# Local attention: inverse norms as a power of -1/2 on GpSimd, one tile at a time; experts' running operations inside the combining loop

## Chip, cores and metric

One core of a Trainium2 chip runs the whole program. The metric is device time in microseconds (us) of one execution. Before the change it is 1561.78 us, the median of three runs (1561.13 to 1563.83).

## What is computed

The input `x` is (2, 1024, 256) in float32. The reference adds two blocks to it:

```python
x = x + experts(attention_0(x, cond), phi, W, b)      # soft mixture of 64 experts, 32 slots each
x = x + two_layers(quaternion_filter(x, cond), ...)   # two layers of local attention + feed-forward
```

In the experts, `combine` is a softmax over all 2048 slots, and the output is `combine @ y`. In each of the two layers, on 8 heads of 64:

```python
q, k, v = split(shift_token(x) @ wqkv)
q = q / clip(norm(q), 1e-12) * qs;  k = k / clip(norm(k), 1e-12) * ksc
q, k = rotary_xpos(q, k)                 # q*cos*scale + rotate_half(q)*sin*scale
sim = 8 * q k^T, in windows of 128 rows with the window before;  x = x + softmax(sim) @ v @ wo
x = x + ffn(layernorm(shift_token(x)))
```

## The kernel before

The program is a chain of stages with semaphores written out by hand; every engine runs a fixed order of instructions. Two stages are touched.

**Experts** (`stage_moe`). A loop of 4 chunks, 512 slots each. The softmax over slots is a running one: each chunk has new maxima (`nmc`), and `fac` is the factor by which what was summed so far is scaled. At the end of a chunk comes the combining loop over 16 tiles of 128 rows. For tile t TensorE (PE) does 12 products `ETs` x `ys` into a bank (L1076) and then 4 transposes of tile t+2 (L1016). ScalarE (ACT) copies those transposed rows (`ETs[0]`, L1118). VectorE (DVE) adds the bank to the running output `O` (L1188) and subtracts to get the low part of tile t+2's rows (`split_rows`, L1166), for which PE waits two tiles later. Between the last split of `ys` (L1175) and this loop DVE does three small running operations on 128x16: `nrun` <- `nmc` (L1182), `dtmp` <- `DEN` x `fac` (L1184), `DEN` <- `dtmp` + `dc` (L1185). `chain` puts a wait behind each for its own end. In the last chunk GpSimd (POOL) leaves the loop of chunks and works on weights of the next stage meanwhile (L1228 to L1242).

**Layers** (`stage_layers`). Attention works on 16 windows ("tiles") of 128 rows per layer, one per slot t, as a pipeline: in slot t PE transposes the rotated rows of tile t-2 (`rows_of`, L1614), makes queries and keys of tile t (L1587, 12 matmuls), scores of t-2 (L1628), transposes the probabilities of t-3 (L1650), projects t-4 (L1669), makes values of t (L1587, 6 matmuls) and applies the probabilities of t-3 (L1660). After queries and keys of tile t: ACT copies (`qkr`, L1816) and squares (`sq`, L1819); DVE sums the squares per head (`ss`, L1991) and multiplies by sines (`sinp`, L1985); POOL multiplies by cosines (`cosines`, L1494), adds (`turn`, L1502) and multiplies by the inverse norms `rn` (`normalised`, L1508). POOL also scales the probabilities (`probabilities`, L1485, two halves of a tile) and, in slots 6 to 11, takes low parts of the feed-forward weights (`low_piece`, L1457).

The inverse norms are made for two tiles at a time, in odd slots: DVE `tensor_scalar_max` (L1994), ACT `norms` with Sqrt (L1829), DVE `reciprocal` in `inverse_norms` (L1999). So `normalised` of an even tile t-1 runs in the odd slot t, behind `turn(t)`, and that of t behind the first half of the probabilities. Sqrt and Exp are in different table sets of ACT; the compiler puts an ACT_TABLE_LOAD at each switch. The first two tiles of layer 0 are done before its pipeline starts, those of layer 1 in the last unit of the feed-forward of layer 0 (`ahead`).

## Time and profile before

| | |
|---|---|
| median of three runs | 1561.78 us |
| the profiled execution | 1562.27 us |
| its span in the trace | 1560.5 us |
| mean granted TensorE clock | 0.988 |
| attention of layer 0 in the trace | about 903 to 1110 us |
| attention of layer 1 | about 1232 to 1454 us |
| combining loop of the last chunk | 832 to 870 us |

The span is one execution from first to last instruction; the profiled execution's own time has 1.8 us around it. "Idle before" is time of an engine in front of an instruction, with the instruction that released it. Starts are in us from the start of the span, durations in us in timelines and in ns as a mean of one in groups.

### The profile page before, as it was taken

To read this page: it belongs to the slowest core of one execution; us is meant where nothing else is said; L and a number is where in the kernel's file an instruction comes from. 1 tells how busy PE (TensorE), PEld (TensorE's weight loads), DVE (VectorE), ACT (ScalarE), POOL (GpSimd) and SP (SyncE) were. 2 spreads that over 40 slices of the span, in tenths; PEclk is the share of its full clock that TensorE was granted. 3 is DMA by queue.
4 is the path that set the end of the run, shared out by engine and by line. 5 is a ranking of instruction groups with operands and counts; after the bars stand their busy time and mean duration, and the time that the engine had idled before them with its cause. 6 is when DMAs were issued, how large, how long until landed. Compare 5 with 4: busy or idle time off the path is not lost. (4 is left out here: it accounts for less than half of the span.)

```text
span 1560.5 us, 24403 instructions
## 1 busy us (share of the span) xinstructions
PE 1470.8 (94%) x9004; PEld 964.0 (62%) x9004; DVE 1024.2 (66%) x1855; ACT 903.1 (58%) x1888; POOL 521.8 (33%) x323
## 2 busy tenths in 40 slices
PE   8889999999998899999998989999999889999998
PEld 3432222222225679797886668777777678777776
DVE  3768888888835446455565656666597566666675
ACT  5137777777784443435242277878543478978341
POOL 7100000000003400000004177887443478887222
PEclk9999999999999999999999999999999999999999
DMA  7920223110000312030304120000200100000010
GB/s 246 162 41 1 42 41 42 22 21 2 1 11 14 125 45 78 13 108 13 108 0 146 41 71 2 2 1 1 74 9 0 58 1 2 1 1 28 14 41 27
DMA packets 59476, 64.84 MB, mean 42 GB/s; under 512 B 15154, under 2 KB 48706, under 8 KB 59380
## 3 DMA queue, kind: packets, MB, share of 16 engines
q1 hardware_dynamic: 58020, 60.17, 15.4%
q10 hardware_dynamic: 1360, 3.41, 0.6%
q8 instruction: 58, 0.95, 0.2%
q14 instruction: 38, 0.31, 0.1%
HBM read 52.88 MB, written 10.49 MB: 41 GB/s over the span
## 5 line engine op out<-in xcount | busy, mean ns | idle before, releaser
L581 DVE TENSOR_REDUCE mcol<-bank 128x1 f32<-128x1024 f32 x256 | 302.1, 1217 | 59.0 <-PE bank L572 59.0
L669 ACT ACTIVATE a_pt<-bank 128x512 f32<-128x512 f32 x512 | 266.4, 602 | 89.2 <-PE bank L701 89.2
L701 PE MATMUL bank<-qa,ka 99*128 99x512 bf16 x512 | 193.7, 386 | 7.6 <-ACT a_pt L669 3.8
L572 PE MATMUL bank<-ka,qa 96*128 96x512 bf16 x512 | 193.2, 385 | 6.3 <-DMA ka<-k_parts 2.9
L2045 DVE CUSTOM_DVE_ANT_0 w_sm<-bank,mask 128x256 f32<-128x256 f32 (+1 forms) x256 | 88.8, 403 | 109.9 <-PE bank L1628 109.9
L1587 PE MATMUL bank<-wqkv,w_hst 128*128 128x512 f32 x576 | 153.6, 412 | 2.7 <-DVE w_sinp L1985 2.3
L701 PEld LDWEIGHTS bank<-qa,ka 99*128 99x128 bf16 x512 | 49.1, 98 | 165.7 <-ACT a_pt L669 121.3
L712 PE MATMUL bank<-a_pt,vst 128*32 128x512 f32 x1024 | 136.4, 605 | 0.1
L1879 ACT ACTIVATE w_sm<-w_sm,w_st 128x256 f32<-128x256 f32 (+1 forms) x256 | 123.9, 488 | 17.8 <-DVE w_st L2045 17.6
L1587 PEld LDWEIGHTS bank<-wqkv,w_hst 128*128 128x128 f32 x576 | 106.8, 193 | 26.6 <-issue 5.1
L1485 POOL TENSOR_TENSOR w_sm<-w_sm,w_st 128x1024 f32<-128x1024 f32 (+1 forms) x64 | 115.4, 1804 | 19.0 <-DVE w_st L2052 18.9
L618 POOL COPY vst<-v 128x512 f32<-128x512 f32 x8 | 4.9, 612 | 336.1 <-PE bank L712 279.6
L1076 PE MATMUL bank<-f_y,f_ET 128*128 128x256 f32 x768 | 110.4, 293 | 6.8 <-DVE f_ET L1166 6.1
L1076 PEld LDWEIGHTS bank<-f_y,f_ET 128*128 128x128 f32 x768 | 97.8, 194 | 10.2 <-DVE f_ET L1166 7.1
L1033 PE MATMUL bank<-phi,X0T 128*128 128x512 f32 x384 | 92.1, 395 | 4.6 <-PEq L768 4.6
L1494 POOL TENSOR_TENSOR w_cosp<-w_qkr,cosT 128x1024 f32<-128x1024 f32 x32 | 76.5, 2392 | 56.8 <-ACT w_qkr L1816 28.4
L1502 POOL TENSOR_TENSOR w_turned<-w_cosp,w_sinp 128x1024 f32<-128x1024 f32 x32 | 76.5, 2389 | 45.7 <-issue 43.1
L1007 PE MATMUL bank<-f_th,X 128*128 128x512 f32 x384 | 90.3, 389 | 0.0
L572 PEld LDWEIGHTS bank<-ka,qa 96*128 96x128 bf16 x512 | 49.8, 99 | 62.7 <-DVE mcol L581 11.3
L1033 PEld LDWEIGHTS bank<-phi,X0T 128*128 128x128 f32 x384 | 72.9, 191 | 20.7 <-issue 5.4
L742 POOL CAST phi<-phi 128x1024 fp32r<-128x1024 f32 x5 | 5.2, 1039 | 240.7 <-PE bank L1033 151.1
L1118 ACT ACTIVATE f_ET<-bank 128x512 fp32r<-128x512 f32 x64 | 37.8, 597 | 81.8 <-PE bank L1016 81.8
(254 smaller groups left out, 2867.2 us busy)
## 6 DMA issues: line engine op xcount, KB each, us to landing
f_wex<-in_W SPq DMA_DIRECT2D x8, 2048.0 KB, 12.0
qa<-q_parts SPq DMA_DIRECT2D x48, 128.0 KB, 4.8
ka<-k_parts SPq DMA_DIRECT2D x48, 128.0 KB, 5.0
q_parts<-p_parts SPq DMA_DIRECT2D x16, 192.0 KB, 3.2
k_parts<-p_parts SPq DMA_DIRECT2D x8, 384.0 KB, 3.4
wqkv_raw<-in_wqkv SPq DMA_DIRECT2D x2, 1536.0 KB, 6.5
w_raw<-in_w SPq DMA_DIRECT2D x2, 1408.0 KB, 5.9
phi<-in_phi SPq DMA_DIRECT2D x5, 512.0 KB, 3.7
```

Source lines behind the costliest of these rows:

```text
L572: last = nc.tensor.matmul(max_bank(G, r)[:, jh * HALF:(jh + 1) * HALF], G["qa"][k][0:KS, hg % 2, h, it * P:(it + 1) * P], G["ka"][k][0:KS, ...
L581: nc.vector.reduce_max(G["mcol"][hg % 2][:, p:p + 1], max_bank(G, r)[:, :], X).then_inc(G["max_free"], 1)
L669: nc.scalar.activation(pt[n % 2][:, q, :], sbank(HG * step + q), ACT.Exp, scale=HD0 ** -0.5).then_inc(p_ready, 1)
L701: mm(sbank(i), ka[k][:, q, n * P:(n + 1) * P], qa[k][:, ih, q, :], start=True, stop=True).then_inc(st_ps, 1)
L712: last = mm(obank[32 * q:32 * q + 32, :], vst[hg // 2 % 2][:, jt, q, :], pt[jt % 2][:, q, :], start=(jt == 0), stop=(jt == TT - 1))
L1007: last = mm(PB[2 + b][:, k * HALF:(k + 1) * HALF], X0[cx][:, b * TT + mt, k * P:(k + 1) * P], ths[ct][:, mt % 2, :], start=(mt == n == 0), ...
L1033: last = mm(logit_bank(mt)[:, b * HALF:(b + 1) * HALF], X0T[cx][:, k, b * T + mt * P:b * T + (mt + 1) * P], phis[cp][:, k, :], start=(n == ...
L1076: last = mm(PB[1][:, HALF * (t % 2):HALF * (t % 2) + D], ETs[ce][:, t % 2, n, :], ys[cy][:, n, t // TT, :], start=(n == i == 0), stop=(n = ...
L1485: V.tensor_tensor(sm[:, i % 2, hs, keys(i)], sm[:, i % 2, hs, keys(i)], st[:, i % 2, 3, hs].unsqueeze(2).to_broadcast([P, 4, 2 * WIN if i ...
L1587: last = mm(out_ps, hst[:, i // 2 % 2, ch, k, (i % 2) * P:(i % 2 + 1) * P], wqkv[cw][:, k, j * INNER:(j + 1) * INNER], start=(n == k == 0) ...
L1879: last = S(sm[:, i % 2, h, keys(i)], sm[:, i % 2, h, keys(i)], ACT.Exp, bias=st[:, i % 2, 1, h:h + 1], scale=-1.0, accum_out=st[:, i % 2, ...
L2045: V.tensor_tensor_reduce(sm[:, s, h, keys(i)], S_PS[h % 2][:, c0:c0 + 2 * WIN][:, keys(i)], mask_of(i), -QK_SCALE, HIGHEST, ALU.add, ALU.m ...
```

## The change

The three running operations of the experts go from in front of the combining loop to a place inside it, behind tile 12's addition and the split of tile 14. In the layers, Sqrt on ACT and the maximum and reciprocal on DVE (for two tiles) go; POOL does a maximum and a power with a constant tensor of -0.5 for each tile, directly behind `turn(t)`, and `normalised(t)` runs in slot t for each tile. DVE's sum of squares now waits that the power of two tiles before is done (`ss` has two buffers).

```diff
--- experts, DVE
                     link = chain(dve, run_step, 3 * c)
-                    dve.wait_ge(run_arg, c + 1)
-                    link(V.tensor_copy(nrun[:, 0, :], nmc[:, :]))
                     dve.wait_ge(run_fac, c + 1)
-                    link(V.tensor_tensor(dtmp[:, :], DEN[:, :], fac[:, :], ALU.mult))
-                    link(V.tensor_tensor(DEN[:, :], dtmp[:, :], dc[:, :], ALU.add))
                     for t in range(TILES):
...
                             split_rows(t + 2)
+                        if t == TILES - 4:
+                            link(V.tensor_copy(nrun[:, 0, :], nmc[:, :]))
+                            link(V.tensor_tensor(dtmp[:, :], DEN[:, :], fac[:, :], ALU.mult))
+                            link(V.tensor_tensor(DEN[:, :], dtmp[:, :], dc[:, :], ALU.add))
--- layers, POOL
+                    def inverse_norms(i):
+                        pool.wait_ge(ss_done, before(i) + 1)
+                        V.tensor_scalar_max(nsq[:, i % 2, :], ss[:, i % 2, :], 1e-24).then_inc(n_square, 1)
+                        pool.wait_ge(n_square, before(i) + 1)
+                        V.tensor_tensor(rn[:, i // 2 % 2, i % 2, :], nsq[:, i % 2, :], exponent[:, :], ALU.pow).then_inc(rn_done, 1)
...
-                        pool.wait_ge(rn_done, NG // 2 * l + i // 2 + 1)
+                        pool.wait_ge(rn_done, before(i) + 1)
...
                             cosines(t)
-                            if t == 1:
-                                normalised(t - 1)
                             turn(t)
-                        if there(t) and t % 2 and t > 1:
-                            normalised(t - 1)
+                            inverse_norms(t)
                         if there(t - 2):
                             probabilities(t - 2, 0)
-                        if there(t) and t % 2:
+                        if there(t):
                             normalised(t)
--- layers, ACT
-                def norms(l, q):
-                    act.wait_ge(n_square, NG // 2 * l + q + 1)
-                    act.wait_ge(rn_done, NG // 2 * l + q)
-                    S(nrm[:, :, :], nsq[:, :, :], ACT.Sqrt).then_inc(n_sqrt, 1)
...
-                        if there(t) and t % 2:
-                            norms(l, t // 2)
--- layers, DVE
                 def squared_norms(l, i):
                     dve.wait_ge(sq_done, NG * l + i + 1)
+                    dve.wait_ge(rn_done, NG * l + max(i - 1, 0))
                     V.reduce_sum(ss[:, i % 2, :], sq[:, :].rearrange("p (h d) -> p h d", d=HD1), X).then_inc(ss_done, 1)
-                    if i % 2:
-                        dve.wait_ge(ss_done, NG * l + i + 1)
-                        V.tensor_scalar_max(nsq[:, :, :], ss[:, :, :], 1e-24).then_inc(n_square, 1)
-
-                def inverse_norms(l, q):
-                    dve.wait_ge(n_sqrt, NG // 2 * l + q + 1)
-                    dve.wait_ge(turn_done, NG * l + max(2 * q - 2, 0))
-                    V.reciprocal(rn[:, q % 2, :, :], nrm[:, :, :]).then_inc(rn_done, 1)
```

POOL's order in slots 4 and 5 of layer 0 before (`w_cosp` is `cosines`, `w_turned<-w_cosp` is `turn`, `w_turned<-w_turned` is `normalised`, `w_sm` is `probabilities`):

```order
L1494 TENSOR_TENSOR w_cosp<-w_qkr,cosT 128x1024 [waits w_add_done,w_qk_sb]
L1502 TENSOR_TENSOR w_turned<-w_cosp,w_sinp 128x1024 [waits w_tk_ps,w_sin_done,w_cos_done]
L1485 TENSOR_TENSOR w_sm<-w_sm,w_st 128x1024 [waits w_d_done] x2
L1494 TENSOR_TENSOR w_cosp<-w_qkr,cosT 128x1024 [waits w_add_done,w_qk_sb]
L1502 TENSOR_TENSOR w_turned<-w_cosp,w_sinp 128x1024 [waits w_tk_ps,w_sin_done,w_cos_done]
L1508 TENSOR_TENSOR w_turned<-w_turned,w_rn 128x1024 [waits w_rn_done,w_add_done]
L1485 TENSOR_TENSOR w_sm<-w_sm,w_st 128x1024 [waits w_d_done]
L1508 TENSOR_TENSOR w_turned<-w_turned,w_rn 128x1024 [waits w_rn_done,w_add_done]
```

and the same two slots now (the first rows of the second slot are those of the first):

```order
L1494 TENSOR_TENSOR w_cosp<-w_qkr,cosT 128x1024 [waits w_add_done,w_qk_sb]
L1502 TENSOR_TENSOR w_turned<-w_cosp,w_sinp 128x1024 [waits w_tk_ps,w_sin_done,w_cos_done]
L1506 TENSOR_SCALAR w_nsq<-w_ss 128x16 [waits w_ss_done]
L1508 TENSOR_TENSOR w_rn<-w_nsq,w_exponent 128x16 [waits w_n_square]
L1485 TENSOR_TENSOR w_sm<-w_sm,w_st 128x1024 [waits w_d_done]
L1514 TENSOR_TENSOR w_turned<-w_turned,w_rn 128x1024 [waits w_rn_done,w_add_done]
L1485 TENSOR_TENSOR w_sm<-w_sm,w_st 128x1024 [waits w_d_done]
```

The even tile's `normalised` moved from the slot after it, behind that slot's `cosines` and `turn`, into its own slot.

DVE's order at the start of the combining loop before:

```order
L1175 TENSOR_TENSOR f_y<-bank,f_y 128x512
L1182 COPY f_nrun<-f_nmc 128x16
L88 ISA
L1184 TENSOR_TENSOR f_dtmp<-den,f_fac 128x16
L88 REGISTER_ALU
L1185 TENSOR_TENSOR den<-f_dtmp,f_dc 128x16
L88 REGISTER_ALU
L1188 SCALAR_TENSOR_TENSOR O<-O,f_fac,bank 128x256
```

and the place of the three operations now, near the loop's end:

```order
L1184 SCALAR_TENSOR_TENSOR O<-O,f_fac,bank 128x256
L1165 REGISTER_ALU
L1166 TENSOR_TENSOR f_ET<-bank,f_ET 128x512
L1190 COPY f_nrun<-f_nmc 128x16
L88 ISA
L1191 TENSOR_TENSOR f_dtmp<-den,f_fac 128x16
L88 REGISTER_ALU
L1192 TENSOR_TENSOR den<-f_dtmp,f_dc 128x16
```

They moved behind 13 of the loop's 16 additions and 13 of its 14 splits.

## Rows read from the trace of the kernel before

**Rows 1.** The page: busy time, share of the span, instructions.

```profile
PE 1470.8 (94%) x9004; PEld 964.0 (62%) x9004; DVE 1024.2 (66%) x1855; ACT 903.1 (58%) x1888; POOL 521.8 (33%) x323
```

**Rows 2.** Timeline of DVE, start of the last combining loop: start, us, instruction, idle before.

```profile
831.97 3.20 DVE L1182 COPY f_nrun<-f_nmc 128x16 f32<-128x16 f32 x1
...
838.58 1.37 DVE L1185 TENSOR_TENSOR den<-f_dtmp,f_dc 128x16 f32<-128x16 f32 x1
...
869.08 0.48 DVE L1188 SCALAR_TENSOR_TENSOR O<-O,f_fac,bank 128x256 f32<-128x256 f32 x1 [1.19 <-PE bank L1076]
```

**Rows 3.** The same of the chunk before: one of three alike, a step, the last addition.

```profile
748.60 0.17 DVE L1184 TENSOR_TENSOR f_dtmp<-den,f_fac 128x16 f32<-128x16 f32 x1
...
772.74 0.69 DVE L1166 TENSOR_TENSOR f_ET<-bank,f_ET 128x512 fp32r<-128x512 f32 x1 [0.59 <-ACT f_ET L1118]
...
777.10 0.48 DVE L1188 SCALAR_TENSOR_TENSOR O<-O,f_fac,bank 128x256 f32<-128x256 f32 x1 [1.20 <-PE bank L1076]
```

**Rows 4.** Timeline of POOL beside the last combining loop.

```profile
831.65 6.86 POOL L1231 TENSOR_TENSOR wqkv<-wqkv_raw,wqkv 128x1536 fp32r<-128x1536 f32 x2
...
844.99 1.28 POOL L1242 TENSOR_TENSOR sinT<-sinT,qks 128x512 f32<-128x512 f32 x1
```

**Rows 5.** Timeline of PE: the loop's start in either chunk.

```profile
748.54 0.62 PE L1076 MATMUL bank<-f_y,f_ET 128*128 128x256 f32 x3 [0.17 <-DVE f_y L1175]
...
832.11 0.63 PE L1076 MATMUL bank<-f_y,f_ET 128*128 128x256 f32 x3 [0.18 <-DVE f_y L1175]
...
841.12 2.93 PE L1076 MATMUL bank<-f_y,f_ET 128*128 128x256 f32 x12 [6.08 <-DVE f_ET L1166]
```

**Rows 6.** All instructions that touch `w_turned`: who waited for it.

```profile
  PE bank L1614: 21.5, 15
```

**Rows 7.** Timeline of PE: slots 3, 4, 16 of layer 0, slots 4, 6, 7 of layer 1.

```profile
921.66 0.66 PE L1660 MATMUL bank<-w_PT,w_vsb 128*64 128x128 f32 x8 [0.85 <-DVE w_PT L2058]
925.25 1.97 PE L1614 MATMUL bank<-ident,w_turned 128*128 128x128 f32 x8 [2.94 <-POOL w_turned L1508]
926.87 4.98 PE L1587 MATMUL bank<-wqkv,w_hst 128*128 128x512 f32 x12
...
1092.50 1.14 PE L1628 MATMUL bank<-w_kT,w_qT 64*128 64x256 f32 x8 [1.67 <-ACT w_qT L1860]
...
1259.15 4.43 PE L1587 MATMUL bank<-wqkv,w_hst 128*128 128x512 f32 x12
...
1286.55 1.09 PE L1614 MATMUL bank<-ident,w_turned 128*128 128x128 f32 x8 [0.96 <-POOL w_turned L1508]
1287.40 3.04 PE L1587 MATMUL bank<-wqkv,w_hst 128*128 128x512 f32 x12
...
1299.47 1.09 PE L1614 MATMUL bank<-ident,w_turned 128*128 128x128 f32 x8
```

**Rows 8.** Busy time by stretch; granted clock is the third number from the end.

```profile
925.00:941.00 16.00, 15.75 (x107) 13.08 (x108) 7.48 (x24) 8.77 (x23) 11.73 (x7) 0.81 0.00 1
```

**Rows 9.** Groups of POOL by line and shape: busy us, mean ns, idle before.

```profile
L1485 POOL TENSOR_TENSOR w_sm<-w_sm,w_st 128x1024 f32<-128x1024 f32 x56 | 106.4, 1900 | 17.6 <-DVE w_st L2052 17.5
L1494 POOL TENSOR_TENSOR w_cosp<-w_qkr,cosT 128x1024 f32<-128x1024 f32 x32 | 76.5, 2392 | 56.8 <-ACT w_qkr L1816 28.4 <-issue 28.4
L1502 POOL TENSOR_TENSOR w_turned<-w_cosp,w_sinp 128x1024 f32<-128x1024 f32 x32 | 76.5, 2389 | 45.7 <-issue 43.1 <-POOL w_cosp L1494 2.2
L1508 POOL TENSOR_TENSOR w_turned<-w_turned,w_rn 128x1024 f32<-128x1024 f32 x32 | 61.9, 1935 | 7.6 <-DVE w_rn L1999 7.4
L1457 POOL TENSOR_TENSOR w<-w_raw,w 128x704 fp32r<-128x704 f32 x8 | 14.4, 1795 | 0.0
...
L990 POOL TENSOR_TENSOR f_bias_rows<-f_bex,f_bias_part 16x256 fp32r<-16x256 f32 x4 | 2.9, 733 | 0.7 <-POOL f_bias_part L987 0.7
...
L975 POOL MEMSET f_nrun<- 128x16 f32 x1 | 0.1, 120 | 0.0
```

**Rows 10.** Groups of ACT from 882 to 1500 us: loads of tables.

```profile
L1829 ACT ACT_TABLE_LOAD x16 | 20.5, 1283 | 0.3
```

More of the change, by code:

```diff
@@ L1273, in stage_layers @@
         nsq = sb("w_nsq", [P, 2, 2 * H1])
-        nrm = sb("w_nrm", [P, 2, 2 * H1])
+        exponent = sb("w_exponent", [P, 2 * H1])
         rn = sb("w_rn", [P, 2, 2, 2 * H1])
@@ L1331, in stage_layers @@
             "step", "on_ready", "t_ps", "x1_done", "rot_ps", "rot_out", "zeroed"))
-        (h_high, h_low, qk_ps, v_ps, qk_sb, v_sb, sq_done, ss_done, n_square, n_sqrt, rn_done) = (sem("w_" + n) for n in (
-            "h_high", "h_low", "qk_ps", "v_ps", "qk_sb", "v_sb", "sq_done", "ss_done", "n_square", "n_sqrt", "rn_done"))
+        (h_high, h_low, qk_ps, v_ps, qk_sb, v_sb, sq_done, ss_done, n_square, rn_done) = (sem("w_" + n) for n in (
+            "h_high", "h_low", "qk_ps", "v_ps", "qk_sb", "v_sb", "sq_done", "ss_done", "n_square", "rn_done"))
         (cos_done, sin_done, add_done, turn_done, tq_ps, tk_ps, qT_done, kT_done, s_ps, s_masked, e_done,
@@ L1535, in _ @@
                 V.memset(eps[:, :], LN_EPS).then_inc(consts, 1)
-                pool.wait_ge(consts, 2)
+                V.memset(exponent[:, :], -0.5).then_inc(consts, 1)
+                pool.wait_ge(consts, 3)
                 attention(0)
@@ L1939, in feed_forward @@
                             round_qkv(l + 1)
-                        if ahead:
-                            norms(l + 1, 0)
                 for n in range(2):
@@ L1949, in _ @@
                         rotated(2)
-                norms(0, 0)
                 rotated(3)
@@ L2086, in attention @@
                             added(t - 4)
-                        if there(t) and t % 2:
-                            inverse_norms(l, t // 2)
                         if there(t - 3):
@@ L2133, in feed_forward @@
                             high(u + 1)
-                        if ahead:
-                            inverse_norms(l + 1, 0)
                         for m in range(KD):
@@ L2165, in _ @@
                 sines(0, 1)
-                inverse_norms(0, 0)
                 attention(0, EARLY_SLOTS)
```

## The prediction

> **What bounds the kernel now.** I read the page first: PE is busy for 94% of the span, no other engine for more than 66% [rows 1], so outside the places where PE stands still nothing is to be gained. The groups of instructions then show who made it stand: two places bear on the change.
>
> The first is the combining loop of the last chunk. The timelines of the two last chunks, side by side, are to be compared. In the third chunk the loop runs from 748.54 (its first product that waits, PE) to 777.10 (last addition of DVE), 28.56 us [rows 3, 5]; in the fourth from 832.11 to 869.08, 36.97 us [rows 2, 5]. The work is the same; 8.41 us are lost once. The reader sees where: the three running operations on 128x16 take 0.17 us each in the third chunk [rows 3], but in the fourth the first alone 3.20 us and all three 7.98 us (831.97 to 839.95) [rows 2]. POOL is at work on large tensors through just that stretch [rows 4], and nobody else is. DVE's next split comes late, and PE waits 6.08 us for it [rows 5]; the other 2.3 us follow while PE comes up to its clock again (12 products take 2.93 us).
>
> The second is the attention. All instructions on `w_turned` show that PE waits 21.5 us in 15 waits for `normalised` [rows 6]. The timeline shows the pattern: slot 6 of layer 1 begins with a wait of 0.96 us, slot 7 with none, and a slot without one is 12.92 us long (1299.47 - 1286.55) [rows 7]. Only even slots wait: the even tile's `normalised` stands on POOL behind `cosines` and `turn` of the tile after it. The slots 4 wait longest, 2.94 us each, and behind that the granted clock is 0.81 for 16 us, between the levels of 1.2 and 2.4 GHz [rows 8]; 12 matmuls take 4.98 us in layer 0 and 4.43 in layer 1, where they take 3.04 at full clock [rows 7].
>
> **Part by part.** The sum is made against the profiled execution, 1562.27 us (span 1560.5); the median is 0.5 lower.
>
> *A, experts: -8.4 us.* At tile 12 of the last loop the time is about 862 - 8, still past POOL's last operation (846.27) [rows 4], so the three take 0.17 each. In the loop DVE idles 0.59 us per tile before a split [rows 3]; three operations with their waits are some 0.6 us, once per chunk. That cover holds them; without it 4 x 0.6 = 2.4 us would be paid. The other DVE operations at the loop's start take one input from PSUM, and the split (0.69) and addition (0.48) show no stretching in either chunk. So the fourth loop becomes like the third: 8.41 us.
>
> The Trainium skill, in "SBUF — State Buffer", on the shared port pair, states that DVE and GpSimd take it as an exclusive lock for a whole instruction, and that DVE needs it for copies in a two-port mode and for two SBUF inputs. By that rule the operations are not slowed in proportion but wait out whole POOL instructions; the trace agrees (3.20 us beside operations of 3.43, 6.86 in two) [rows 2, 4], and the rule too frees them at the new place. It also says that the new small POOL instructions can be held up by DVE, which I price below from rows.
>
> *B, waits of PE for `normalised`: -21.5 us* [rows 6]. By the new order an even tile is ready about a whole slot earlier: in slot t `turn` ends, then come the norm, 1.90 of probabilities and 1.94 of `normalised` [rows 9], and PE wants it only two slot starts after its own slot began. That is a margin of some 10 us. What is late next is not this tile but the probabilities, under E.
>
> *C, clock: -4.5 us.* With the waits of 2.94 us gone the clock has nothing to fall for: 12 matmuls 4.98 - 3.04 and 4.43 - 3.04, the transposes ahead of them 1.97 - 1.09 and, in layer 1, some 0.3 [rows 7]: 1.94 + 0.88 + 1.39 + 0.3.
>
> *D, ACT and DVE: -3.3 us.* 16 groups of Sqrt lose a table load of 1.28 us each [rows 10] and 15 the load back; nearly all of the 40 us lie beside PE's work and give nothing. On the path are two places: DVE waits for the Sqrt in slot 3 and copies probabilities late, for which PE waits 0.85 us in each layer [rows 7], 1.7; and in slot 16, where PE has no projections to hide ACT's copies, it waits 1.67 us for `w_qT` [rows 7], of which I take half, 0.8 per layer, as ACT's backlog of exponentials and loads.
>
> *E, POOL's new work: +8.0 us.* Per tile a maximum and a power on 128x16. The trace has no power. Lower bound for each: 0.12 us, the memset of 128x16. Upper bound for the power: 1.94 us, a multiplication of 128x1024, that is, as if each of the 16 numbers took 64 plain operations. A short operation of two inputs with 256 columns takes 0.73 [rows 9]; I take 0.7 for the power, as it is nearest in kind, 0.12 for the maximum, and 0.17 for the wait between them (0.7 us of idle in 4 before L990). Together 1.0 us per tile. POOL's slot is then 2 x 1.90 + 2.39 + 2.39 + 1.94 = 10.5, now 11.5 us [rows 9]: hidden under 12.9. In slots 6 to 11 a low part (1.80) comes on top, 13.3 us against 12.9: 6 x 0.4 = 2.4. The first tile of the second sequence has one window of keys instead of two, which shortens PE's slot there more than POOL's; I add 1.2 for it and take 1 off for the margin that PE leaves before it wants the second half of the probabilities: 2.6 us per layer (an estimate). Slots 2 and 3 are short on PE and POOL is the slower one there; two norms push the probabilities of tile 1 some 1.4 us past PE's need: 1.4 per layer. So 2 x 4.0. With the power at 0.12 the whole of E is about 1 us; at 1.94 the excess of 1.24 counts in those six slots and the first two: 2 x (4.0 + 8 x 1.24), about 28.
>
> DVE's maximum and reciprocal (0.5 us for two tiles) go from beside PE's work: nothing. The new wait of the sum of squares is for a power two slots back: nothing, unless the power is of a slot's length. POOL's memset of the exponent is 0.12 us where POOL idles.
>
> Sum: -8.4 - 21.5 - 4.5 - 3.3 + 8.0 = -29.7; 1562.3 - 29.7 = 1532.6, or 1532 as a median.
>
> **The rivals.**
>
> *The power is long, slower (0.18).* The Q7 cores may do it in a loop per number. POOL's slot becomes 10.8 us + p, with p the power. Up to p = 2.1 it hides in the eight plain slots of a layer; from there every slot is POOL's. The cost per layer is by E 4.0 + 8 (p - 0.7), and 8 (p - 2.1) more above 2.1. What it has to use up is half of A to D, 18.9 us: 15.2 at p = 2.1, the rest at 16 us per us, so the turn is at p = 2.3. With p = 4 it is 45.6 per layer: 91 - 38 = 53 us over before, 1616. For it speaks that no row shows such a function; against it that all POOL rows show whole vectors of partitions at 1.9 to 2.3 ns a column, and 16 columns are few.
>
> *The power eats the gain (0.12).* p of 1.4 to 2.3, hidden in plain slots only: at 1.8, E is 2 x 12.8 = 25.6, and 12 us are left, 1550.
>
> *The next wait takes over (0.15).* PE no longer gives the other engines 1 us per pair of slots. `turn` waits for the sines ("issue", 43.1 us of POOL's idle [rows 9]), which stand on DVE behind sum of squares and maxima; the scores' maxima come after PE. If half of B and C return: 1562.3 - 8.4 - 13 - 3.3 + 4 = 1541.6.
>
> *The first power pays for its code (0.05).* In this trace no first use of an operation on POOL shows as longer. If code is fetched at the first norm of layer 0, it falls ahead of PE's first wish for tile 0, and at most some 6 us of B's and A's gain is lost once: 1538. The Trainium skill, "GPSIMD Engine Reference", on instruction dispatch, gives about 6 us for the first call to a freshly loaded kernel, without a visible instruction; by it the sum would be 1538 too. No row here bears it out, hence the small chance.
>
> *The running operations stay slow (in the chance of the take-over).* If not POOL but something of the last chunk stretches them, they would cost their 8 us at tile 12, and the time is 1541.
>
> **How the numbers follow.** My forecast, 1532, has 0.50; take-over 0.15, first call 0.05, eaten 0.12, slower 0.18. Its own range is 1524 (power at 0.12, E about 1) to 1541. The range of 8 in 10 adds the eaten case: 1523 to 1557. What is left out is the long power above all. A measurement of this kernel can tell some 0.2% (3 us) from no change. Faster by more: 0.50 + 0.15 + 0.05 + 0.09 of the eaten, 0.79; within 0.04; slower 0.17.
>
> **What the profile after would show.** Right: the fourth combining loop 28.6 us long, its three operations 0.17 each; the power near 0.7 us; hardly any wait of PE for `w_turned`; a granted clock of 1.0 behind slot 4; no Sqrt table loads in the slots; small waits of PE for POOL's probabilities in slots 6 to 11. Wrong: a power of 2 us or more, with POOL busy through every slot and PE waiting for `w_sm`; or PE's waits unchanged in sum under another name, the sines or the maxima; or slow running operations with POOL idle.

## The result and the profile after

| | before | after |
|---|---|---|
| median | 1561.45 us (1559.97 to 1563.83, 4 runs) | 1589.19 us (1588.47 to 1594.31, 4 runs) |
| profiled execution | 1562.27 us, span 1560.5 | 1588.72 us, span 1586.6 |
| ratio | | 1.0182, 95% interval 1.0165 to 1.0199 |

The changed kernel is 1.8% slower; 1532 was forecast, and the range ended at 1557.

The page of the changed kernel: POOL has 106 us more work than in [rows 1], ACT 38 us less, and the chain that ended last now runs through POOL for 17% of the span, where it was 4%; `w_rn`, the power, is in it with 4%.

```profile
PE 1473.6 (93%) x9004; PEld 964.1 (61%) x9004; DVE 1014.1 (64%) x1823; ACT 865.5 (55%) x1841; POOL 627.7 (40%) x388
...
PE 18%; POOL 17%; DVE 7%; issue 3%; ACT 1%; POOLq 0%; DVEq 0%
```

Groups of POOL by line and shape (busy us, mean ns of one, idle before), against [rows 9]: the large products cost what they did; the power costs 3.10 us in the mean, 99.2 us in 32, and the maximum 0.34.

```profile
L1508 POOL TENSOR_TENSOR w_rn<-w_nsq,w_exponent 128x16 f32<-128x16 f32 x32 | 99.2, 3101 | 2.7
L1514 POOL TENSOR_TENSOR w_turned<-w_turned,w_rn 128x1024 f32<-128x1024 f32 x32 | 60.8, 1900 | 0.6
L1506 POOL TENSOR_SCALAR w_nsq<-w_ss 128x16 f32<-128x16 f32 x32 | 10.9, 342 | 0.1
```

Timeline of POOL through one slot of layer 0 (start, us, instruction): no operation waits for anything, each begins where the last one ends. From one `cosines` to the next it is 15.25 us, where TensorE needs 12.92 for a slot [rows 7]. It is a slot with a piece of the feed-forward weights' low part (`w<-w_raw`); slots without one are 13.6 to 14.2 us long between 920 and 1110 us, so they too are longer than TensorE's.

```profile
1000.16 2.37 POOL L1494 TENSOR_TENSOR w_cosp<-w_qkr,cosT 128x1024 f32<-128x1024 f32 x1
1002.61 2.37 POOL L1502 TENSOR_TENSOR w_turned<-w_cosp,w_sinp 128x1024 f32<-128x1024 f32 x1
1004.96 0.25 POOL L1506 TENSOR_SCALAR w_nsq<-w_ss 128x16 f32<-128x16 f32 x1
1005.29 2.92 POOL L1508 TENSOR_TENSOR w_rn<-w_nsq,w_exponent 128x16 f32<-128x16 f32 x1
1008.19 1.89 POOL L1485 TENSOR_TENSOR w_sm<-w_sm,w_st 128x1024 f32<-128x1024 f32 x1
1010.04 1.90 POOL L1514 TENSOR_TENSOR w_turned<-w_turned,w_rn 128x1024 f32<-128x1024 f32 x1
1011.90 1.69 POOL L1457 TENSOR_TENSOR w<-w_raw,w 128x704 fp32r<-128x704 f32 x1
1013.56 1.89 POOL L1485 TENSOR_TENSOR w_sm<-w_sm,w_st 128x1024 f32<-128x1024 f32 x1
1015.41 2.35 POOL L1494 TENSOR_TENSOR w_cosp<-w_qkr,cosT 128x1024 f32<-128x1024 f32 x1
```

Busy time by stretch, PE, PEld, DVE, ACT, POOL in this order: POOL fills 117.00 of 120 and 98.87 of 100 us of layer 0's slots and 117.03 of 120 in layer 1, PE 103 to 105 of 120.

```profile
880.00:1000.00 120.00, 103.18 (x734) 80.38 (x732) 69.03 (x190) 76.60 (x192) 117.00 (x61) 0.99 0.08 27
1000.00:1100.00 100.00, 87.06 (x695) 70.71 (x696) 56.13 (x168) 68.38 (x173) 98.87 (x53) 0.98 0.00 1
...
1340.00:1460.00 120.00, 104.68 (x852) 85.18 (x850) 69.36 (x204) 83.62 (x213) 117.03 (x63) 0.99 0.01 1
```

What PE waited for (us in total, times, longest). The 21.5 us for the rotated and normalised rows [rows 6] have gone to 1.3, and 49.6 us for POOL's probabilities stand there instead:

```profile
PE bank L1654 <- POOL w_sm L1485: 49.6, 38, 4.6
PE bank L1752 <- DVE w_sinp L1979: 5.2, 1, 5.2
```

The experts' part did what was forecast. The last combining loop starts at 830.95 on PE and its last addition at 859.50 on DVE, 28.55 us instead of 36.97 [rows 2, 5], and the three running operations take 0.17 each (timeline of DVE):

```profile
855.76 0.16 DVE L1190 COPY f_nrun<-f_nmc 128x16 f32<-128x16 f32 x1
855.96 0.18 DVE L1191 TENSOR_TENSOR f_dtmp<-den,f_fac 128x16 f32<-128x16 f32 x1
856.17 0.17 DVE L1192 TENSOR_TENSOR den<-f_dtmp,f_dc 128x16 f32<-128x16 f32 x1
...
859.50 0.48 DVE L1184 SCALAR_TENSOR_TENSOR O<-O,f_fac,bank 128x256 f32<-128x256 f32 x1 [1.19 <-PE bank L1076]
```

### The profile page after: what moved, and what is told of

It is laid out like the page before. It is cut to its first block and busy times, and to the rows that moved or that the text cites. A ratio compares the mean times of both kernels' runs of the same rounds, so it can differ in the third digit from the quotient of the medians.

```text
span 1586.6 us, 24390 instructions
## 1 busy us (share of the span) xinstructions
PE 1473.6 (93%) x9004; PEld 964.1 (61%) x9004; DVE 1014.1 (64%) x1823; ACT 865.5 (55%) x1841; POOL 627.7 (40%) x388
## 5 line engine op out<-in xcount | busy, mean ns | idle before, releaser
L1485 POOL TENSOR_TENSOR w_sm<-w_sm,w_st 128x1024 f32<-128x1024 f32 (+1 forms) x64 | 114.9, 1795 | 9.5 <-DVE w_st L2038 9.5
L1654 PE MATMUL bank<-ident,w_sm 128*128 128x128 f32 x480 | 67.4, 283 | 49.6 <-POOL w_sm L1485 49.6
L1508 POOL TENSOR_TENSOR w_rn<-w_nsq,w_exponent 128x16 f32<-128x16 f32 x32 | 99.2, 3101 | 2.7
L1654 PEld LDWEIGHTS bank<-ident,w_sm 128*128 128x128 f32 x480 | 54.2, 143 | 68.9 <-POOL w_sm L1485 65.9
L572 PEld LDWEIGHTS bank<-ka,qa 96*128 96x128 bf16 x512 | 49.7, 99 | 61.2 <-DVE mcol L581 11.3
## 6 DMA issues: line engine op xcount, KB each, us to landing
f_wex<-in_W SPq DMA_DIRECT2D x8, 2048.0 KB, 11.8
```

The costliest lines, as they stand in the source:

```text
L572: last = nc.tensor.matmul(max_bank(G, r)[:, jh * HALF:(jh + 1) * HALF], G["qa"][k][0:KS, hg % 2, h, it * P:(it + 1) * P], G["ka"][k][0:KS, ...
L1485: V.tensor_tensor(sm[:, i % 2, hs, keys(i)], sm[:, i % 2, hs, keys(i)], st[:, i % 2, 3, hs].unsqueeze(2).to_broadcast([P, 4, 2 * WIN if i ...
L1508: V.tensor_tensor(rn[:, i // 2 % 2, i % 2, :], nsq[:, i % 2, :], exponent[:, :], ALU.pow).then_inc(rn_done, 1)
L1654: last = tr(T_PS[p % 2][:, c0:c0 + P], sm[:, i % 2, 2 * p + e, j * P:(j + 1) * P], ident[:, :])
```

## The experiments

The theory after the first look: **the power is long.** It takes 2.9 to 3.3 us where 0.7 was taken, POOL becomes the bound of both layers' slots, and terms A to D of the sum stand. The rivals: the order itself costs (the norm stands ahead of the probabilities on POOL); only the lateness of one product counts and not POOL's sum of work; something in the experts' part. Times are medians of runs beside the kernel before on the same chip; its own median was 1562.41, 1560.38, 1562.09 and 1562.37 us in the four sets of runs.

### Each part alone

`e1_moe_only` has only the experts' part of the change, the layers as before. Against the kernel before:

```diff
-                    dve.wait_ge(run_arg, c + 1)
-                    link(V.tensor_copy(nrun[:, 0, :], nmc[:, :]))
...
+                        if t == TILES - 4:
+                            link(V.tensor_copy(nrun[:, 0, :], nmc[:, :]))
```

> Only the experts' part of the change: the three running operations inside the combining loop. Theory (term A): the fourth loop lost 8.4 us to POOL's large operations, so 1561.4 - 8.4 = 1553. Rival: what is saved there is waited for behind it (tables, loads of the next stage), and the time stays at 1558 or more.

Measured: 1555.45 us (1552.70 to 1558.69), ratio 0.9956 (0.9936 to 0.9975). That is 7.0 us less than the kernel before; term A was 8.4, and the spread of the runs covers the difference. The loop itself is 28.55 us long here too (831.71 to 860.26 us). In the profiled execution the lead is 9.2 us at the first wait for `w_PT` in layer 0 (912.41 against 921.66) and 6.9 where layer 1's slots end (1446.78 against 1453.63), so some of it may be waited for behind the loop, as the rival has it; one trace can't tell that from chance. PE's waits for the rotated rows are as before:

```profile
PE bank L1614 <- POOL w_turned L1508: 21.3, 15, 2.9
```

`e2_layers_only` has only the layers' part; against the changed kernel:

```diff
+                    dve.wait_ge(run_arg, c + 1)
+                    link(V.tensor_copy(nrun[:, 0, :], nmc[:, :]))
...
-                        if t == TILES - 4:
-                            link(V.tensor_copy(nrun[:, 0, :], nmc[:, :]))
```

> Only the layers' part of the change. If the parts add up, 1589.2 + 8.4 = 1597.6. If the experts' part is worth less than its 8.4 us, this comes out nearer to 1590.

Measured: 1596.03 us (1595.79 to 1596.37), ratio 1.0214 (1.0197 to 1.0231), 33.6 us more than before. The two parts add up: -7.0 + 33.6 = 26.6 against 27.7 for the whole. The loss is the layers' alone.

### The power made short

`e3_mult`:

```diff
-                        V.tensor_tensor(rn[...], nsq[...], exponent[:, :], ALU.pow).then_inc(rn_done, 1)
+                        V.tensor_tensor(rn[...], nsq[...], exponent[:, :], ALU.mult).then_inc(rn_done, 1)
```

> The changed kernel with the power replaced by a multiplication of the same shape, 128x16 (the norms are then not the inverse ones; all else is as in the change). Theory 1, the length of the power alone is the loss (2.93 us instead of the 0.7 taken), and the terms A to D stand: with some 0.15 us in its place POOL hides everything, 1561.4 - 37.7 + 1 = about 1525, at most 1530. Theory 2, the new order itself costs (norms, probabilities and products in one slot make PE wait for something else): 1541 or more.

Measured: 1529.39 us (1526.96 to 1530.82), ratio 0.9787 (0.9769 to 0.9804). One operation code is 60 us. (This run leaves out the inverse norms; it measures time only.) The groups of POOL and the waits of PE in this run:

```profile
L1508 POOL TENSOR_TENSOR w_rn<-w_nsq,w_exponent 128x16 f32<-128x16 f32 x32 | 10.8, 337 | 2.7
```

```profile
PE bank L1632 <- ACT w_qT L1859: 4.4, 5, 1.1
...
PE bank L1654 <- POOL w_sm L1485: 1.9, 3, 0.8
```

The order, the semaphores and the number of operations are those of the changed kernel; the waits of PE for `w_sm` fall from 49.6 to 1.9 us, and there is none for `w_turned`. The rival that the order itself costs falls. It also measures the other terms: the sum without E was 1562.3 - 37.7 = 1524.6, and E was about 1 us with a power of 0.12; the two small operations take 0.63 here.

### POOL's sum of work, or the lateness of one product?

`e7_power_later` has the same work in another place of the slot:

```diff
                             turn(t)
-                            inverse_norms(t)
                         if there(t - 2):
                             probabilities(t - 2, 0)
                         if there(t):
+                            inverse_norms(t)
                             normalised(t)
```

> The changed kernel with maximum and power moved behind the probabilities of the tile before, directly ahead of the normalised product: the same work on GpSimd, but its other products come out 3.2 us earlier in a slot. If GpSimd's sum of work is the bound (its slot of some 14 to 15 us against TensorE's 12.9), the order inside a slot moves nothing beyond a few us: 1580 to 1595 us. If it is only the lateness of the first product of a slot (what TensorE waits for is one operation late, GpSimd itself has time to spare), the time falls clearly, to 1545 to 1570 us.

Measured: 1597.56 us (1592.98 to 1599.03), ratio 1.0234 (1.0217 to 1.0251). The first probabilities of a slot come 3 us earlier and the kernel is no faster, rather half a per cent slower; what I had said it would at most reach was 1595. Lateness of that product alone falls. PE's waits for `w_sm` are nearly the same in sum, 45.6 us, but in 24 pieces instead of 38, and PE is busy 9.0 us longer (1482.6 against 1473.6) with the same 9004 products at a lower granted clock (0.981 against 0.987). That the longer single waits cost the clock is a reading and not shown.

`e4_power_twice` writes each power twice into the same place:

```diff
+                        V.tensor_tensor(rn[...], nsq[...], exponent[:, :], ALU.pow).then_inc(n_square, 1)
+                        pool.wait_ge(n_square, 2 * before(i) + 2)
                         V.tensor_tensor(rn[...], nsq[...], exponent[:, :], ALU.pow).then_inc(rn_done, 1)
```

> The changed kernel with each power computed twice into the same place, 2.9 us more in every slot and nothing else. If GpSimd's sum of work is the bound of both layers' slots, all 28 to 32 further powers are paid in full: 81 to 93 us, so 1670 to 1682 us. If the changed kernel's loss is one of order, with room left on GpSimd, part of it is hidden: below 1650 us.

Measured: 1670.11 us (1668.83 to 1672.78), ratio 1.0694 (1.0676 to 1.0712): 80.9 us more than the changed kernel for 32 further powers of 2.91 in the mean (93 us). By the waits of PE:

```profile
PE bank L1656 <- POOL w_sm L1485: 98.7, 30, 5.5
PE bank L1620 <- POOL w_turned L1516: 8.0, 2, 6.1
```

So nearly nine tenths of the further work on POOL are paid. The theory of the bound stands.

### Where does the price begin?

`e11_half` multiplies for even tiles and takes the power for odd ones:

```diff
-                        V.tensor_tensor(rn[...], nsq[...], exponent[:, :], ALU.pow).then_inc(rn_done, 1)
+                        V.tensor_tensor(rn[...], nsq[...], exponent[:, :],
+                                        ALU.pow if i % 2 else ALU.mult).then_inc(rn_done, 1)
```

> The changed kernel with a multiplication in place of the power for even tiles, so that their inverse norms are not computed, and the power for odd ones alone: the mean of the two is (0.22 + 2.93) / 2 = 1.58 us. If GpSimd's slot decides only from where it passes TensorE's 12.9 us (its work then 10.5 + 0.25 + 1.58 = 12.3 us, with a piece of the experts' low part in 9 of 16 slots 13.2), the time lies nearer to the 1529 us of the run with multiplications alone than to the changed kernel's 1589: 1538 to 1550. If each us of the power costs the same, it lies halfway: 1557 to 1561.

Measured: 1555.01 us (1553.45 to 1558.92), ratio 0.9961 (0.9949 to 0.9972). That lies between the two forecasts and settles nothing by itself. (The expectation counts pieces of a low part in 9 of 16 slots; they are pieces of the feed-forward weights, in slots 6 to 11, so in 6.) `e15_four_columns` therefore spreads a like amount evenly:

```diff
+                        V.tensor_tensor(rn[..., 4:], nsq[..., 4:], exponent[:, 4:], ALU.mult).then_inc(n_square, 1)
+                        pool.wait_ge(n_square, 2 * before(i) + 2)
-                        V.tensor_tensor(rn[...], nsq[...], exponent[:, :], ALU.pow).then_inc(rn_done, 1)
+                        V.tensor_tensor(rn[..., :4], nsq[..., :4], exponent[:, :4], ALU.pow).then_inc(rn_done, 1)
```

> The changed kernel with the power on 4 of each tile's 16 columns alone and a multiplication for the other 12, whose inverse norms are not computed. From the two sizes of the power seen (2.93 us for 16 columns, 5.46 for 32: 0.40 and 0.158 a column) it takes 1.03 us, with 0.2 to 0.6 for the multiplication 1.2 to 1.7 in every slot: about the mean work of the run with the power for odd tiles alone (1.72 us a slot, 1555 us), but spread evenly. If a slot is paid for only where GpSimd's work in that very slot passes TensorE's 12.9 us (here 12.0 to 12.6, there 14 in every second), the time is 1532 to 1545 us. If the time goes by the amount of work alone, it is 1550 to 1560 us.

Measured: 1542.61 us (1541.22 to 1546.34), ratio 0.9880 (0.9863 to 0.9897), within the forecast for work that is paid slot by slot. With the groups of both runs the five kernels of this order can be laid on a line. First `e11_half`, then `e15_four_columns`:

```profile
L1508 POOL TENSOR_TENSOR w_rn<-w_nsq,w_exponent 128x16 f32<-128x16 f32 x32 | 54.9, 1715 | 2.7
L1506 POOL TENSOR_SCALAR w_nsq<-w_ss 128x16 f32<-128x16 f32 x32 | 9.8, 307 | 0.0
```

```profile
L1510 POOL TENSOR_TENSOR w_rn<-w_nsq,w_exponent 128x4 f32<-128x4 f32 x32 | 33.5, 1046 | 2.5
L1508 POOL TENSOR_TENSOR w_rn<-w_nsq,w_exponent 128x12 f32<-128x12 f32 x32 | 12.0, 374 | 2.7
L1506 POOL TENSOR_SCALAR w_nsq<-w_ss 128x16 f32<-128x16 f32 x32 | 10.2, 318 | 0.1
```

| kernel | small operations per tile, us | time, us | us paid in all per us added to each slot |
|---|---|---|---|
| multiplications | 0.63 | 1529.4 | |
| power of 4 columns | 1.74 | 1542.6 | 12 (from 0.63) |
| power for odd tiles | 2.02 | 1555.0 | |
| as changed | 3.44 | 1589.2 | 27 (from 1.74) |
| power twice | 6.25 | 1670.1 | 29 (from 3.44) |

There are 32 slots with a tile, so 32 would be the whole price. From 1.74 us a slot on each further us is paid 27 times in the mean, from 3.44 on 29 times; below 1.74 only 12 times, so there is some room. If added work were free up to a point and had that price behind it, the point would be 1.74 - 13.2 / 28 = 1.3 us (an estimate): 10.5 + 1.3 = 11.8 us of work on POOL, before gaps and waits, against TensorE's 12.9. The slots are not alike, though, and it is a mean: a slot with a piece (1.80) has 12.9 - 10.5 - 1.8 = 0.6 us of room, one without has 2.4 (estimates from [rows 7, 9]). How much the even spread does is less clear: `e11_half` has 0.28 us more work in a slot, which at 27 us per us is 8 of the 12.4 us between the two (14.1, if each is held against its own kernel before); the other 4 to 6 may be due to work that comes in every second slot.

### One power for two tiles

`e8_two_tiles` takes one power of 128x32 in each odd slot, as the square root did before the change:

```diff
-                            inverse_norms(t)
+                            if t % 2:
+                                inverse_norms(t // 2)
+                                normalised(t - 1)
                         if there(t - 2):
                             probabilities(t - 2, 0)
-                        if there(t):
+                        if there(t) and t % 2:
                             normalised(t)
```

> The changed kernel with the inverse norms of two tiles in one power of 128x32 in each odd slot, 16 of them instead of 32, both normalised products behind it. If the power's price is one of each element (2.93 us for 16 columns, so 0.18 us a column), the new power takes 5.7 to 5.9 us, GpSimd has as much work as before, but all of it in odd slots: 1585 to 1605 us. If the price is one of each instruction, the power takes 3 to 3.5 us and 16 of 2.93 us go, which takes GpSimd's mean slot from some 14 to 12.4 us: 1535 to 1560 us.

Measured: 1675.96 us (1672.83 to 1681.47), ratio 1.0745 (1.0720 to 1.0770). The price is one of each element: 5.48 us for 32 columns. But the time lies 71 us above the upper end forecast. The groups and the waits say why:

```profile
L1508 POOL TENSOR_TENSOR w_rn<-w_nsq,w_exponent 128x32 f32<-128x32 f32 x16 | 87.6, 5476 | 1.3
```

```profile
PE bank L1620 <- POOL w_turned L1514: 112.0, 15, 9.4
```

POOL has even less work than in the changed kernel (612.7 against 627.7 us busy) and fills only 84 of 100 us in the slots (1010 to 1110). Now it is lateness: the even tile's product waits behind `cosines` and `turn` of the next tile and a power of 5.5 us, and PE stands for it up to 9.4 us in every second slot. So the mechanism of the kernel before [rows 6] comes back larger. In PE's timeline, the wait and the projections behind it, 3.76 us instead of 3.04 [rows 7]:

```profile
1032.68 1.97 PE L1620 MATMUL bank<-ident,w_turned 128*128 128x128 f32 x8 [6.73 <-POOL w_turned L1514]
1034.30 3.76 PE L1593 MATMUL bank<-wqkv,w_hst 128*128 128x512 f32 x12
```

### The norms on other engines

`e12_sqrt_per_tile` keeps POOL's new order and puts the square root back on ACT and maximum and reciprocal on DVE, for each tile:

```diff
+                def norms(l, i):
+                    act.wait_ge(n_square, NG * l + i + 1)
+                    S(nrm[:, i % 2, :], nsq[:, i % 2, :], ACT.Sqrt).then_inc(n_sqrt, 1)
...
+                def inverse_norms(l, i):
+                    dve.wait_ge(n_sqrt, NG * l + i + 1)
+                    V.reciprocal(rn[:, i // 2 % 2, i % 2, :], nrm[:, i % 2, :]).then_inc(rn_done, 1)
```

> The changed kernel's order on GpSimd (one tile a slot, product right ahead of the probabilities) with the experts' small operations early, but the square root on ScalarE and maximum and reciprocal on VectorE as before, once for each tile and not for two. GpSimd's slot is then 10.5 us and has time to spare. ScalarE loads its tables twice in each slot instead of in every second: 32 further loads of 1.28 us less those that startup shares, some 1.3 us more a slot, on a ScalarE that is busy 0.58 of the span. If ScalarE has the room, the time is that of the run with multiplications plus the clock and the table loads at its edge: 1530 to 1540 us. If the square root, late in ScalarE's order, is what TensorE then waits for, it is 1545 us or more.

Measured: 1546.85 us (1544.06 to 1547.15), ratio 0.9901 (0.9883 to 0.9919). The expectation of 1530 to 1540 was missed, the rival's bound of 1545 reached, but TensorE does not wait for the norms themselves. ACT loads tables 62 times in the slots, 79.6 us, and PE waits for its copies 8.1 us and 3.1, where it was 4.4 with the multiplication. That is 7 of the 17.5 us between the two kernels; PE is also busy 9.7 us longer (1471.7 against 1462.0), at a granted clock of 0.985 against 0.992:

```profile
L1875 ACT ACT_TABLE_LOAD x32 | 41.1, 1283 | 0.6
L1825 ACT ACT_TABLE_LOAD x30 | 38.5, 1283 | 0.5
```

```profile
PE bank L1624 <- ACT w_qT L1856: 8.1, 5, 2.4
...
PE bank L1624 <- ACT w_kT L1860: 3.1, 1, 3.1
```

`e10_swap` leaves the norms as they were before the change (two tiles, ACT and DVE) and only puts the even tile's product ahead of `turn` in every odd slot; it has the experts' part too:

```diff
                             cosines(t)
-                            if t == 1:
+                            if t % 2:
                                 normalised(t - 1)
                             turn(t)
-                        if there(t) and t % 2 and t > 1:
-                            normalised(t - 1)
```

> The experts' part, and in the layers the old Sqrt and reciprocal for two tiles, but in odd slots the even tile's product ahead of turn(t) instead of behind it. Theory: PE's 15 waits for that product are a matter of POOL's order; it ends 2.4 us earlier, the waits of 0.96 us go and those of 2.94 shrink to some 0.6, and the clock stays up: 1553 less 15 to 20 us, 1533 to 1538. Rival: Sqrt's result is there no earlier than turn could have ended, or the probabilities behind it come too late; then 1545 or more.

Measured: 1543.47 us (1541.99 to 1544.41), ratio 0.9877 (0.9861 to 0.9893). It beats both kernels and is the fastest version here that computes everything, with `e12_sqrt_per_tile` close behind; 1533 to 1538 was not reached. Against `e1_moe_only` the move of one product is worth 12.0 us. Waits of PE: 7.3 of the 21.3 us are left, as POOL itself now waits for the reciprocal (at 1015.69 for 2.25 us; in all 47.5 us in 16 waits, up to 5.8, where it was 7.4 [rows 9]), and 3.6 us for POOL's probabilities are new.

```profile
PE bank L1612 <- POOL w_turned L1508: 7.3, 9, 1.7
```

```profile
1015.69 1.90 POOL L1508 TENSOR_TENSOR w_turned<-w_turned,w_rn 128x1024 f32<-128x1024 f32 x1 [2.25 <-DVE w_rn L1997]
```

`e14_newton` computes the inverse norms on DVE without a root: a first value from the number's bits, a step of Newton's and one of third order.

```diff
+                    step(V.tensor_scalar(y.bitcast(I32), x.bitcast(I32), -0.5, 1597463007.0, ALU.mult, ALU.add))
+                    step(V.tensor_tensor(h, y, y, ALU.mult))
+                    step(V.scalar_tensor_tensor(out=h, in0=h, scalar=-0.5, in1=x, op0=ALU.mult, op1=ALU.mult))
...
+                    V.scalar_tensor_tensor(out=rn[...], in0=z, scalar=1.875, in1=y, op0=ALU.add, op1=ALU.mult)
```

> The changed kernel's order with the inverse norms on VectorE alone and without any square root: the maximum, a first value from the bits of the number, one step of Newton's and one of third order, 10 operations on 128x16 for each tile, at 0.1 to 0.2 us each some 1 to 2 us of VectorE in a slot (it is busy 0.65 of the span). GpSimd keeps its 10.5 us a slot, ScalarE has no square root and no change of tables. If VectorE has the room, the time is that of the run with multiplications, 1527 to 1540 us. If its operations wait for GpSimd's (the maximum took 0.61 us in the mean where it stood on VectorE beside GpSimd's products), 10 of them cost 6 us or more a slot and VectorE becomes the bound: above 1560 us.

Measured: 1648.39 us (1646.71 to 1652.42), ratio 1.0559 (1.0541 to 1.0577), a loss of 119 us against the multiplications. DVE's own work grew by 118 us (1132.1 against 1014.1), but the wait is elsewhere: the ten operations stood ahead of the sum `xr`, and PE waited for it.

```profile
L1995 DVE TENSOR_TENSOR w_newton<-w_newton 128x16 f32<-128x16 f32 x32 | 68.7, 2147 | 1.1
L1996 DVE SCALAR_TENSOR_TENSOR w_newton<-w_newton,w_nsq 128x16 f32<-128x16 f32 x32 | 7.7, 241 | 1.1
```

```profile
PE bank L1657 <- DVE xr L2067: 65.0, 24, 3.2
```

`e16_newton_last` moves them to the end of DVE's slot:

```diff
                             sines(l, t)
-                            inverse_norms(l, t)
...
                             maxima(t - 2, 1)
+                        if there(t):
+                            inverse_norms(l, t)
```

> The version with Newton's steps on VectorE, where the ten operations cost 119 us against the run with multiplications (1648 against 1529 us), now at the end of VectorE's slot, behind the second row maxima, where it waits 3.1 to 4.3 us for TensorE in each slot of the run with multiplications, and no longer ahead of the sum and the copy for which TensorE waited 65 us. The work is the same: 9 operations of 0.17 us and one of about 2.2 us, 4 us a slot. If the loss was the place, most of it comes back: 1530 to 1555 us. If it was the amount (VectorE's slot too full, or GpSimd slowed), it stays above 1570 us.

Measured: 1568.67 us (1566.68 to 1569.10), ratio 1.0040 (1.0025 to 1.0054). 80 of the 119 us come back with the same work, so most of the loss was the place; 39 stay, which neither forecast had. Against the multiplications PE's waits are 22.6 us more in sum (79.8 against 57.2) and its own work is 15.0 us longer (1477.0 against 1462.0, granted clock 0.983 against 0.992). They go with a DVE that is busy for 82% of the slots (1010 to 1110) and hands POOL its work late: POOL waits 11.3 us there for the inverse norms and 7.5 for the sums of the probabilities. PE waits for POOL's probabilities again, POOL filling only 77%:

```profile
1010.00:1110.00 100.00, 93.11 (x764) 76.24 (x762) 82.39 (x243) 70.96 (x185) 76.73 (x40) 0.97 0.00 1
```

```profile
PE bank L1647 <- POOL w_sm L1486: 17.0, 13, 2.3
```

## Why the prediction was wrong

*A, experts, -8.4: right.* The loop is 28.55 us long, like that of the chunk before it [rows 3, 5]. Alone it gives 7.0 us in the median, with an interval of some 4 to 10.

*B, waits for the normalised rows, -21.5: right.* 1.3 us are left in the changed kernel, none with the multiplication.

*C, the clock, -4.5: right where nothing takes the place of the waits.* In the stretch of [rows 8], 925 to 941 us, the run with multiplications has a granted clock of 1.00 (third number from the end) with PE busy for all of its 16 us:

```profile
925.00:941.00 16.00, 16.00 (x136) 13.36 (x133) 8.87 (x30) 12.24 (x35) 15.38 (x12) 1.00 0.01 2
```

In the changed kernel it falls at other places, behind the new waits: the longest, ahead of the transposes of the first tile's probabilities, leaves 6 projections at 2.82 us, which elsewhere take 1.65 (timeline of PE); the granted clock from 909 to 913 us is 0.57.

```profile
909.17 1.11 PE L1654 MATMUL bank<-ident,w_sm 128*128 128x128 f32 x4 [4.60 <-POOL w_sm L1485]
909.94 2.82 PE L1591 MATMUL bank<-wqkv,w_hst 128*128 128x512 f32 x6
...
1012.76 1.65 PE L1591 MATMUL bank<-wqkv,w_hst 128*128 128x512 f32 x6
```

*D, ACT and DVE, -3.3: right by the waits.* ACT lost 37.6 us of work. Waits of PE for `w_qT` are 4.4 us where they were 6.0, and the two of 0.85 for `w_PT` [rows 7] are gone, 1.6 and 1.7 as forecast. A to D together were to give 37.7; the run with multiplications gave 33.0 in the median with 0.63 us of small operations a slot. If these cost by the slope of 12 us per us, they are some 7 us and the four terms gave 40; if they are hidden, the terms gave 33 (estimates). The forecast lies between.

*E, POOL's new work, +8.0: this is the step that failed,* and in it one number, the power, "0.7 us, as it is nearest in kind". It takes 2.92 to 3.33 us, 3.10 in the mean. The maximum took 0.34 where 0.12 was said, the wait between the two 0.08 (2.7 us in 32) where it was 0.17; together 3.5 us a tile, not 1.0, and E cost some 65 us, not 8.0 (an estimate: 27.7 + 37.7, with A to D as forecast). The upper bound was wrong as well: 1.94 us was the time of 1024 columns of multiplication, "as if each of the 16 numbers took 64 plain operations". Nothing in the trace of before carried that sentence; a plain operation is no bound for one of another kind. The sentence on all POOL rows at 1.9 to 2.3 ns a column is not quite so either: in [rows 9] the low part takes 2.5 (1795 ns for 704) and the rows of 256 columns 2.9. The range was built on this bound and left out the case that came.

The rest of E was right in sum, and so was the formula of the rival "the power is long, slower", which had 0.18. With the mean power of 3.10 us it says 2 x (4.0 + 8 x 2.4 + 8 x 1.0) = 62.4, and 1562.3 - 37.7 + 62.4 = 1587.0; the profiled execution took 1588.7. From the multiplication's 0.34 us to 3.10 it says 60.2, and 59.8 were measured. That it meets the sum is in part luck: it pays 16 us per us up to p = 2.1 and 32 above. From p = 0.34 to the 1.42 of `e15_four_columns` that says 17.3 us and 13.2 were measured; from 1.42 to 3.10 it says 42.9 and 46.6 were measured; the two errors cancel. Its turn, p = 2.3, fits the runs: the kernel with 1.72 us in the mean is 0.4% faster than before, that with 3.10 is 1.8% slower.

Of the other rivals, *the power eats the gain* asked for p of 1.4 to 2.3. *The next wait takes over* did not come at all with a short power: 1529.4, with one wait of 3.3 us for the sines as the longest in the layers. *The first power pays for its code* doesn't show: the first power starts at 884.12 and takes 3.33 us, as 13 later ones do within 0.02. The Trainium skill's "GPSIMD Engine Reference" gives about 6 us for a first call, in its section on instruction dispatch; no run here shows it for this operation.

The fault in the chances: an operation without a row, 32 times on an engine that had 2.4 us of room in a slot, was given a price of a third of that room and a chance of 0.30 for more. What spoke for a short one, that 16 columns are few beside 1024, was about the width of the data, not about the operation. The profile's own sign of being wrong came as written down: a power above 2 us, POOL busy through every slot, PE waiting for `w_sm`.

## What to carry to other kernels

Price a function that the trace has never shown by what it would have to cost to turn the result, and give that a chance of its own; a multiplication of any width is no upper bound for a power. A cheap-looking edit on a helper engine is safe only up to that engine's room in a slot: here some 1.3 us in the mean, and beyond it each us added to every one of 32 slots came back as 27 to 29. Edits that come in one change should be weighed apart: the reordering of a product (12 us in `e10_swap`) needed neither the power nor its place on POOL.

## What the runs showed of the hardware

- A power on POOL, f32, with 128 partitions and the exponent -0.5, takes 1.03 us for 4 columns, 2.92 for 16 and 5.46 for 32 at its undisturbed best, which is 0.40 us and 0.158 a column; in the same place and for 16 columns a multiplication takes 0.22. The cost is by the element, so two tiles in one instruction save only the 0.40.
- Short operations of POOL carry 0.40 us more at some places, the power 3.33 instead of 2.92 and the multiplication 0.62 instead of 0.22. In the changed kernel 14 powers take 3.31 to 3.33 us, and each of them starts 0.15 to 0.17 us behind the start of a DVE operation on two tensors in SBUF (0.69 us); the other 18 take 2.92 to 2.93, and none of them starts so. The Trainium skill, "SBUF — State Buffer", on the shared port pair, states that such an instruction and one of GpSimd hold the pair in turn; by that rule POOL waits at its start, and the trace agrees: POOL and DVE of the changed kernel below, where the power is 3.33; at 1005.29, in the timeline of POOL above, the power has no such neighbour and takes 2.92.

```profile
1020.69 3.33 POOL L1508 TENSOR_TENSOR w_rn<-w_nsq,w_exponent 128x16 f32<-128x16 f32 x1
```

```profile
1020.53 0.69 DVE L1969 TENSOR_TENSOR w_hst<-xr,w_hst 128x512 fp32r<-128x512 f32 x1
```

- The same does not hold the other way round for the power. Three such DVE operations start inside a power of POOL (at 1065.04, 1224.23 and 1418.46 us) and take 0.68 to 0.69 us as ever; that the power had the port pair for its whole length, as that rule would have it, is not what this trace shows. Beside large products of POOL they are stretched, to 1.67 us and up to 2.76 (at 902.23). One of the three, POOL and DVE:

```profile
1064.85 2.92 POOL L1508 TENSOR_TENSOR w_rn<-w_nsq,w_exponent 128x16 f32<-128x16 f32 x1
1065.04 0.68 DVE L2010 TENSOR_TENSOR n_sqsum<-n_sq 128x512 f32<-128x512 f32 x1
```

- Ten small operations of DVE in a row are held up once, not ten times: nine of them take about 0.17 to 0.24 us and one 2.15 in `e14_newton`, and where they stand later in the slot it is the first, second or third that is long (means of 0.95, 1.25 and 0.43), again some 2 us in all for a tile.
